# Attention and mixture-of-experts layer on one core: the value block at index 1 of each batch goes from one full-precision product to three rounded ones

## Chip, cores and metric

The kernel runs on one core of a Trainium2 chip (trn2). The metric is device time in microseconds (us); lower is better. Several executions of a kernel are timed and their median is taken. One further execution is profiled, and all rows below come from it.

## What is computed

The input `x` is 2 batches of 1024 tokens with 256 features (2048 tokens). Attention has 4 key/value groups with 4 query heads each, head size 128, rotary embedding and a causal mask. After it come a residual add and a layer norm, then a mixture of 64 experts (6 per token) with one shared expert, a residual add and a second layer norm. Cut to what matters here:

```python
q = einsum('bim,ghmd->bghid', x, w_aq); k = einsum('bim,gmd->bgid', x, w_ak)
v = einsum('bim,gmd->bgid', x, w_av)
s = einsum('bghid,bgjd->bghij', rope(q) * m, rope(k) * m) - 1e30 * (i < j)
o = einsum('bghij,bgjd->bghid', softmax(s), v)
x1 = layernorm(x + einsum('bghid,ghdm->bim', o, w_ao))
ids, w = grouped_topk(sigmoid(x1 @ gate_w) + bias)      # 6 of 64 experts
y = sum_k w_k * expert_k(x1) + silu(x1 @ ws_gate) * (x1 @ ws_up) @ ws_down
out = layernorm(x1 + y)
```

## The kernel before

**Stages.** Projections run from 0 to about 150 us: `x` is transposed, and each 128x512 piece of q, k and v is the sum of six rounded products (`ring`, `s_ps` and `o_ps` from `w_two` and `xt_hi`/`xt_lo`). q and k are rotated with two DVE products and one POOL instruction per piece, and stored to DRAM. Attention runs to about 915 us, then the experts and the final sum to 1071 us.

**Two precisions.** An fp32 operand can go through TensorE as it is (a product that the profile shows as two matmul records, here the line `L1143`), or be split into a rounded half (`_hi`, type fp32r, made by ACT in the helper at L875) and the rest (`_lo`, made by DVE in the helper at L1253 or by POOL). Three products of halves, hi by hi, lo by hi, hi by lo (`PASSES`), then stand for the full one.

**Attention in units.** A tile is 128 query tokens; there are 16 tiles, 8 to a batch. A unit is one tile and one group, so there are 64 units, numbered u = 4 x tile + group. A unit of tile i sees `blocks(u)` = i mod 8 + 1 blocks of 128 keys, and has 4 heads. For each head, PE makes the scores (`s_ps`), DVE takes their maximum (`neg_max`, L1319), ACT the exponential (`probs`, L961). For each key block j, the step (u, j) transposes the four heads' probabilities on PE (L1126, "ptrans") into a bank of `ring`, takes the bank out, and multiplies by the value block (L1143 or L1146, "pv") into `o_ps`, which holds one unit's sum. When the last block is in, DVE multiplies `o_ps` by the inverse row sums into `ot` (L1340, "omul"). There is one `o_ps` bank: the first pv of unit u waits until the omul of unit u-1 has read it (`o_ready`).

**The constant VF.** Value blocks j < VF = 2 of each batch are kept in full precision (`v0`, `v1`): ACT copies the transposed probabilities to `pt` (L972), that copy releases the bank, and PE makes the one full product (L1143). Blocks j >= VF have rounded halves in `v`: ACT makes `pt_hi`, DVE makes `pt_lo` (L1253), and the DVE instruction releases the bank; PE makes three products (L1146).

**The order.** `schedule()` writes one list of steps for all engines, and each engine walks it in order and issues its own part of each step. A step (u, j) is put in the list five heads behind the scores. `waiting` holds LAG = 2 pv steps: as soon as a third is in, the oldest is emitted. So this is emitted at the point that matters for u >= 1, j = 1:

```python
seq.append(("ptrans", u, j))       # (u, 1)
waiting.append((u, j))
if len(waiting) > LAG:
    product()                      # ("pv", u-1, last), and behind it ("omul", u-1)
```

Behind it come the scores of the next head, ptrans (u, 2), and pv (u, 0) (for a unit of two blocks ptrans (u+1, 0) in place of (u, 2)). For units with five or more blocks, steps (u, 0) and (u, 1) belong to one head, and the exponential of the head whose scores came just before is emitted between them; with two to four blocks (u, 1) stands before the exponential.

**Other work in the list.** The router, shared expert and norms of the previous tiles are put between heads by the table `BETWEEN`. The raw router and shared-expert weights wait in the memory of `v1` until they are split (`MISC_AT`). Values of the second batch are stored to DRAM during the projections (`v_out` to `v_rows`), loaded into `v` when the first batch is done with it (`load_v`, four loads, at omul 29 to 32), and split by ACT and POOL (`vsplit`, L829 on POOL). Expert weights are loaded during the second batch into the memory that `kt0`, `v0` and `kt1` leave (`load_homes`).

Of the kernel before, what the change touches and what calls it, by code (L numbers as in the profile page):

```python
# [10 lines left out]
F32 = mybir.dt.float32  # L11
# [4 lines left out]
P = 128  # L16

B, T, M = 2, 1024, 256
G, H, D = 4, 4, 128
NT = T // P  # L20
# [35 lines left out]
RING = 3  # L56
XB = 4
QB = 3
VF = 2
VS = NT - VF  # L60
PRE_BANKS = 8
BLOCKS = ["K", 0, 1, 2, 3, "V"]
# [200 lines left out]
PT_ALL = len(PT_AT)  # L263
PS_AT = {k: n for n, k in enumerate(k for k in PT_AT if k[1] >= VF)}
PROJ_AT = {s: n for n, s in enumerate(s for s in SEQ if s[0] in ("proj", "projv"))}
# [16 lines left out]
def build(nc, x, w_aq, w_ak, w_av, w_ao, gate_w, bias, w_gate, w_up, w_down, ws_gate, ws_up, ws_down,  # L282
# [9 lines left out]
    with ExitStack() as ctx:  # L292
        def sb(name, shape, dt, where=ctx):
            return where.enter_context(nc.sbuf_tensor(name, shape, dt))

        def sem(name):
            return ctx.enter_context(nc.semaphore(name))
# [22 lines left out]
        wsd_lo = sb("wsd_lo", [F, M], F32R)  # L320

        att = ExitStack()
        kt = [sb("kt0", [P, G, 2, T], F32R, att)]
        v_sb = [sb("v0", [P, G, VF, D], F32, att)]
        raw = ExitStack()
# [49 lines left out]

        v_sb.append(sb("v1", [P, G, VF, D], F32, att))
        x_sb = sb("x_sb", [P, XB, M], F32, att)
# [57 lines left out]
        wmisc_lo_ready = sem("wmisc_lo_ready")  # L435
# [110 lines left out]
            return tile.rearrange("p (y h d) -> p y h d", h=H, d=D // 2)  # L546

        kt_hi, kt_lo = [z[:, :, 0, :] for z in kt], [z[:, :, 1, :] for z in kt]
        raw_misc = v_sb[1][:, :, :, :].rearrange("p g n d -> p (g n d)")
        raw_r = raw_misc[:, 0:2 * M].rearrange("p (c n) -> p c n", c=MC)  # L550
        raw_d = raw_misc[0:F, 2 * M:3 * M]

# [2 lines left out]
        def load_k(eng, b, g):  # L555

            for z in range(2):
                eng.dma_start(kt_lo[b][z * D // 2:(z + 1) * D // 2, g, :].bitcast(F32),
                              rows_of[0, z, g * D // 2:(g + 1) * D // 2, b * T:(b + 1) * T]).then_inc(k_loaded, 16)

        def rope_done(eng, c, name):

            for n in range(2 * SETS):
                eng.wait_ge(rope_stored[n], 16 * len(range(n // 2, ropes_until(c, name), SETS)))
# [4 lines left out]
        def read(eng, step):  # L569

            r, turn = PLACE[step]
            eng.wait_ge(ring_read[r], turn + 1)

        def reader(ins, step):

            ins.then_inc(ring_read[PLACE[step][0]], 1)

        def bank(step):
            r = PLACE[step][0]
            if r < 4:  # L580
                return s_ps[:, r // 2, r % 2 * 512:r % 2 * 512 + 512]
            return o_ps[:, :] if r == 4 else ring[:, (r - 5) % RING, :]
# [4 lines left out]
        def used(eng, semaphore, n):  # L587

            if n > 0:
                eng.wait_ge(semaphore, n)  # L590
# [25 lines left out]
        def _(sp):  # L616
# [63 lines left out]
            for s in SEQ:  # L680
# [10 lines left out]
                if s[0] == "score" and s[1:] in K_LOAD_AT:  # L691
                    load_k(sp, 1, K_LOAD_AT.index(s[1:]))
                if s[0] == "projv" and s[1] >= NT + VF:
                    j = s[1] - NT - VF
                    read(sp, s)
# [176 lines left out]
        def _(act):  # L872
            def split(hi, raw):

                return act.activation(hi, raw, ACT.Copy)  # L875
# [10 lines left out]
            for s in SEQ:  # L886
                for name in HIGH_AT.get(s, []):
                    n = BLOCKS.index(name)
# [19 lines left out]
                if kind == "projv":  # L908
                    act.wait_ge(proj_ready, PROJ_AT[s] + 1)
                    b, j = divmod(s[1], NT)  # L910
                    rows = bank(s).rearrange("p (g d) -> p g d", g=G)
                    if j < VF:
                        if s[1] == NT:
                            act.wait_ge(wmisc_lo_ready, 2)
                        reader(act.activation(v_sb[b][:, :, j, :], rows, ACT.Copy), s)
                    elif b == 0:
                        split(v[:, :, 0, j - VF, :], rows).then_inc(v_hi_ready, 1)
                    else:
                        used(act, v_stored, 16 * (j - VF))
                        reader(act.activation(v_out[:, :], bank(s), ACT.Copy), s)  # L920
                if kind == "vsplit":
                    g = s[1]
                    act.wait_ge(v_loaded[g % 2], 16 * (g // 2 + 1))
                    split(v[:, g, 0, :, :], v[:, g, 1, :, :].bitcast(F32)).then_inc(v_later_hi, 1)
                if kind == "ksplit":
                    b, g = s[1:]
                    act.wait_ge(k_loaded, 32 * G * (b + 1))
                    split(kt_hi[b][:, g, :], kt_lo[b][:, g, :].bitcast(F32)).then_inc(k_hi_ready, 1)
                if kind == "proj" and s[1:] in BLANK_AT:
                    n = BLANK_AT.index(s[1:])  # L930
# [5 lines left out]
                if kind == "proj" and s[1] == CHUNKS // B - 1 and s[2] in (1, 2) and s[4] == 1:  # L936
                    rope_done(act, s[1], "K")
                    act.wait_ge(proj_ready, PROJ_AT[s] + 1)
                    load_k(act, 0, 2 * (s[2] - 1) + s[3])
                if s == ("proj", CHUNKS - 1, 1, 0, 0):  # L940
                    act.wait_ge(proj_ready, PROJ_AT[("proj", CHUNKS - 1, 0, 1, 1)] + 1)
# [10 lines left out]
                if kind == "exp":  # L952
                    u, h = s[1:]
                    n = u * H + h
# [9 lines left out]
                if kind == "ptrans":  # L964
                    n = PT_AT[s[1:]]
# [590 lines left out]
```

## Time and profile before

| | us |
|---|---|
| median of 3 runs | 1075.36 |
| lowest and highest of them | 1070.57, 1077.23 |
| the profiled execution's own time | 1073.27 |
| its span, first to last instruction | 1071.5 |
| mean granted TensorE clock in it | 0.957 of full |

The span leaves 1.8 us of the profiled execution's time outside, and that execution was 2.1 us faster than the median. In the rows, PE is TensorE's matmuls, DVE is VectorE, ACT is ScalarE, POOL is GpSimd. Matmuls overlap in the pipeline, so a step's cost on PE is read from start to start. What stands in brackets behind a row is idle time of the engine before it and what ended it.

### The profile page before, as it was taken

How to read it: one execution, taken by the hardware profiler on the slowest of the kernel's cores; microseconds unless marked ns; L12 is line 12 of the kernel's file. 1: busy time of each engine (PE TensorE's matmuls, PEld its weight loads, DVE VectorE, ACT ScalarE, POOL GpSimd, SP SyncE). 2: the span in 40 equal slices, each digit the busy share in tenths (PEclk: the TensorE clock that was granted, in tenths of full speed). 3: DMA queues.
4: the chain of work that ended last, by engine and by line, in shares of the span. 5: the costliest groups of instructions: out<-in, count | busy, mean ns of one | idle time of the engine just before them, and what ended most of it. 6: DMA issues, size and time to landing. Idle time of an engine off the chain costs nothing.

```text
span 1071.5 us, 16751 instructions
## 1 busy us (share of the span) xinstructions
PE 965.9 (90%) x5240; PEld 739.3 (69%) x5240; DVE 681.1 (64%) x1703; ACT 488.6 (46%) x1083; POOL 371.8 (35%) x334
## 2 busy tenths in 40 slices
PE   8999979989999999999979999999999998559745
PEld 6888867667787778776767667888787776336412
DVE  5989853775766675757565668575857666424326
ACT  4012124555656564645544456564645544125402
POOL 4878863234323121021244332312031112126811
PEclk9999988999999999999979999999999999769968
DMA  8696765463222111111243224351112133978687
GB/s 254 228 289 218 250 230 159 127 165 110 73 64 61 60 52 58 45 33 50 85 133 90 84 74 132 87 156 45 56 31 69 44 79 99 274 214 194 86 279 284
DMA packets 137303, 137.24 MB, mean 128 GB/s; under 512 B 18065, under 2 KB 108805, under 8 KB 137216
## 3 DMA queue, kind: packets, MB, share of 16 engines
q1 hardware_dynamic: 84064, 98.33, 30.1%
q10 hardware_dynamic: 43872, 29.50, 9.4%
q0 software_dynamic: 9280, 8.34, 4.5%
q8 instruction: 44, 0.72, 0.3%
q14 instruction: 43, 0.35, 0.1%
HBM read 86.44 MB, written 63.05 MB: 140 GB/s over the span
## 4 chain that ended last, share of the span: by engine, by line
PE 67%; DVE 10%; issue 8%; SPq 5%; DMA 5%; ACT 2%; POOL 2%; ACTq 1%; DVEq 0%; POOLq 0%
PE s_ps L1116 14%; PE ring L1126 9%; PE o_ps L1146 8%; PE o_ps L1143 8%; PE ring L1155 7%; PE s_ps L1095 6%; PE ring L1095 5%; DVE neg_max L1319 2%; SPq L759 2%; PE s_ps L1209 2%; PE o_ps L1095 2%; SPq L655 1%; PE s_ps L1119 1%; DVE pt_lo L1253 1%; DMA inverses<-inv_t 1%
## 5 line engine op out<-in xcount | busy, mean ns | idle before, releaser
L1319 DVE TENSOR_REDUCE neg_max<-s_ps 128x1 f32<-128x128 f32 (+7 forms) x256 | 191.6, 750 | 137.6 <-PE s_ps L1119 131.8
L961 ACT ACTIVATE probs<-s_ps,neg_max 128x128 f32<-128x128 f32 (+7 forms) x256 | 189.7, 741 | 142.3 <-DVE neg_max L1319 127.8
L1116 PE MATMUL s_ps<-kt,qt_hi 128*128 128x512 f32 (+3 forms) x768 | 235.2, 388 | 6.0 <-ACT probs L961 3.9
L824 POOL TENSOR_TENSOR qt_lo<-q_raw,qt_hi 128x512 fp32r<-128x512 f32 x64 | 82.1, 1283 | 319.3 <-ACT qt_hi L875 319.0
L1126 PE MATMUL ring<-ident,probs 128*128 128x128 f32 x1152 | 177.5, 277 | 9.2 <-DVE pt_lo L1253 5.1
L875 ACT ACTIVATE pt_hi<-ring 128x512 fp32r<-128x512 f32 x168 | 99.8, 596 | 181.8 <-PE ring L1126 173.6
L1116 PEld LDWEIGHTS s_ps<-kt,qt_hi 128*128 128x128 f32 x768 | 139.7, 194 | 54.9 <-issue 30.2
L1253 DVE TENSOR_TENSOR pt_lo<-ring,pt_hi 128x512 fp32r<-128x512 f32 x168 | 115.4, 687 | 62.2 <-ACT pt_hi L875 56.7
L1126 PEld LDWEIGHTS ring<-ident,probs 128*128 128x128 f32 x1152 | 129.1, 142 | 33.7 <-issue 14.5
L1146 PE MATMUL o_ps<-pt_hi,v 128*128 128x512 f32 x336 | 145.9, 435 | 1.4 <-DVE pt_lo L1253 0.9
L1116 PE MATMUL s_ps<-kt,qt_lo 128*128 128x512 f32 (+3 forms) x384 | 134.6, 350 | 0.0
L1143 PE MATMUL o_ps<-pt,v 128*128 128x512 f32 x240 | 127.8, 615 | 1.9 <-DVE ot L1340 1.7
L846 POOL DMA_INDIRECT slot_rows<-row,slot_u x96 | 95.1, 990 | 95.7 <-DVE slot_u L1444 73.5
L814 POOL TENSOR_TENSOR prods<-prods 128x512 f32<-128x512 f32 x80 | 108.6, 1385 | 36.6 <-DVE prods L1306 36.2
L1155 PE MATMUL ring<-wo,ot 128*128 128x256 f32 x512 | 113.1, 379 | 0.0
L1155 PEld LDWEIGHTS ring<-wo,ot 128*128 128x128 f32 x512 | 97.1, 190 | 17.5 <-issue 4.3
L972 ACT ACTIVATE pt<-ring 128x512 f32<-128x512 f32 x120 | 71.3, 594 | 26.4 <-PE ring L1126 20.0
L1116 PEld LDWEIGHTS s_ps<-kt,qt_lo 128*128 128x128 f32 x384 | 74.1, 193 | 8.4
L1340 DVE TENSOR_TENSOR ot<-o_ps,inv_row 128x512 f32<-128x512 f32 x64 | 43.9, 686 | 42.4 <-PE o_ps L1146 20.8
L1146 PEld LDWEIGHTS o_ps<-pt_hi,v 128*128 128x128 f32 x336 | 63.4, 189 | 9.5 <-DVE pt_lo L1253 1.7
L1146 PE MATMUL o_ps<-pt_lo,v 128*128 128x512 f32 x168 | 65.8, 392 | 0.0
L833 POOL TENSOR_TENSOR rstd<-var_eps,minus_half 128x1 f32<-128x1 f32 x16 | 9.1, 569 | 153.2 <-DVE var_eps L1352 153.2
(201 smaller groups left out, 1378.8 us busy)
## 6 DMA issues: line engine op xcount, KB each, us to landing
qk_rows<-prods SPq DMA_DIRECT2D x80, 256.0 KB, 2.8
q_raw<-qk_rows ACTq DMA_DIRECT2D x128, 128.0 KB
inv_row<-inverses SPq DMA_DIRECT2D x64, 256.0 KB
fsum<-sums SPq DMA_DIRECT2D x48, 256.0 KB, 8.1
sums<-blank SPq DMA_DIRECT2D x16, 640.0 KB
wexp<-in_L_ffn_w_gate_dram SPq DMA_DIRECT2D x32, 192.0 KB, 5.0
wexp<-in_L_ffn_w_up_dram SPq DMA_DIRECT2D x32, 192.0 KB, 5.2
wexp<-in_L_ffn_w_down_dram SPq DMA_DIRECT2D x32, 192.0 KB, 6.3
```

Of the source, the lines that this page charges most:

```text
L814: pool.tensor_tensor(pair[:, z, 0, :], pair[:, z, 0, :], pair[:, z, 1, :], op).then_inc(rot_ready, 1)
L846: pool.indirect_dma_start(slot_rows[:, :], bass.IndirectOffsetOnAxis(ap=slot_u[:, i % 2, k:k + 1], axis=0), row[:, i % 2, :], None, bounds ...
L875: return act.activation(hi, raw, ACT.Copy)
L961: act.activation(probs[:, u % 2, h, 0:blocks(u) * P], s_ps[:, n % 2, score_cols(n)], ACT.Exp, bias=neg_max[:, n % 8:n % 8 + 1], accum_out= ...
L1095: ins = pe.matmul(bank(s), *sides, start=(turn == 0), stop=(turn == len(PROJ_PASSES) - 1))
L1116: pe.matmul(s_ps[:, n % 2, c + a:c + e], q[qp], k[kp][:, a:e], start=(qp == kp == 0), stop=(qp == 1 and not last))
L1126: ins = pe.transpose(bank(s)[:, h * P:(h + 1) * P], probs[:, u % 2, h, j * P:(j + 1) * P], ident[:, :])
L1143: ins = pe.matmul(o_ps[:, :], v_sb[i // NT][:, g, j, :], pt[:, n % PTB, :], start=first, stop=last)
L1146: ins = pe.matmul(o_ps[:, :], v[:, g, vp, j - VF, :], (pt_hi, pt_lo)[pp][:, n % PTB, :], start=False, stop=(last and vp == 1))
L1155: ins = pe.matmul(bank(s)[:, 0:M], ot[:, h // H, (h % H) * P:(h % H + 1) * P], wo[:, h, :], start=(h == 0), stop=(h == G * H - 1))
L1253: return dve.tensor_tensor(lo, raw, hi.bitcast(F32), ALU.subtract)
L1319: dve.tensor_reduce(neg_max[:, n % 8:n % 8 + 1], s_ps[:, n % 2, score_cols(n)], AX_X, ALU.max, negate=True).then_inc(max_ready, 1)
```

## The change

`VF` becomes 1. Only value block 0 of each batch stays in full precision; block 1 is made of rounded halves and goes through the three products, as blocks 2 to 7 do. `v` holds seven blocks for each group in place of six, `v0` and `v1` one in place of two. `v1` is then too small for the raw router and shared-expert weights, so these are loaded into a tensor of their own that lies in the memory of `kt0`; the loads of the first batch's keys into `kt0` wait until the weights have been split, and the first copy into `v1` no longer does.

```diff
-VF = 2
+VF = 1
 VS = NT - VF
...
         att = ExitStack()
+        early = ExitStack()
+        raw_misc = sb("raw_misc", [P, 3 * M], F32, early)
+        early.close()
         kt = [sb("kt0", [P, G, 2, T], F32R, att)]
         v_sb = [sb("v0", [P, G, VF, D], F32, att)]
...
-        raw_misc = v_sb[1][:, :, :, :].rearrange("p g n d -> p (g n d)")
         raw_r = raw_misc[:, 0:2 * M].rearrange("p (c n) -> p c n", c=MC)
...
                     if j < VF:
-                        if s[1] == NT:
-                            act.wait_ge(wmisc_lo_ready, 2)
                         reader(act.activation(v_sb[b][:, :, j, :], rows, ACT.Copy), s)
...
                     rope_done(act, s[1], "K")
                     act.wait_ge(proj_ready, PROJ_AT[s] + 1)
+                    act.wait_ge(wmisc_lo_ready, 2)
                     load_k(act, 0, 2 * (s[2] - 1) + s[3])
```

The rest follows from `VF`. The lines of `build` behind the new ones stand a line lower after the change (L1253 is then L1254, L1340 is L1341).

**PE, unit 27.** The transposes of blocks 2 and 3 (`ring<-ident,probs`) and the products of blocks 0 and 1 (`o_ps<-...`) behind them. Before:

```order
1120 L1126 MATMUL ring<-ident,probs 128x128 x4
1121 L1143 MATMUL o_ps<-pt,v0 128x512
1122 L1126 MATMUL ring<-ident,probs 128x128 x4
1123 L1143 MATMUL o_ps<-pt,v0 128x512
1124 L1180 MATMUL ring<-chose,before_bf 128x64
```

The same place after the change:

```order
1166 L1127 MATMUL ring<-ident,probs 128x128 x4
1167 L1144 MATMUL o_ps<-pt,v0 128x512
1168 L1127 MATMUL ring<-ident,probs 128x128 x4
1169 L1147 MATMUL o_ps<-pt_hi,v 128x512
1170 L1147 MATMUL o_ps<-pt_lo,v 128x512
1171 L1147 MATMUL o_ps<-pt_hi,v 128x512
1172 L1181 MATMUL ring<-chose,before_bf 128x64
```

The product of block 1 is three instructions in place of one, at the same place.

**DVE, between units 26 and 27.** `neg_max` are score maxima, `inv_sum` and `inv_t` the inverse row sums of unit 27, `ot` the omul of unit 26, `chose_s` to `row` routing work. Before:

```order
615 L1319 TENSOR_REDUCE neg_max<-s_ps 128x1
616 L1325 RECIPROCAL inv_sum<-row_sum 128x4
617 L1326 STREAM_TRANSPOSE inv_t<-inv_sum 128x32
618 L1340 TENSOR_TENSOR ot<-o_ps,inv_row 128x512
619 L1415 SCALAR_TENSOR_TENSOR chose_s<-left,sig 128x64
620 L1418 TENSOR_REDUCE top_sum<-chose_s 128x1
621 L1419 RECIPROCAL top_inv<-top_sum 128x1
622 L1420 TENSOR_SCALAR row<-chose_s,top_inv 128x64
623 L1319 TENSOR_REDUCE neg_max<-s_ps 128x1
624 L1253 TENSOR_TENSOR pt_lo<-ring,pt_hi 128x512 x2
```

The same place after the change:

```order
641 L1320 TENSOR_REDUCE neg_max<-s_ps 128x1
642 L1326 RECIPROCAL inv_sum<-row_sum 128x4
643 L1327 STREAM_TRANSPOSE inv_t<-inv_sum 128x32
644 L1254 TENSOR_TENSOR pt_lo<-ring,pt_hi 128x512
645 L1341 TENSOR_TENSOR ot<-o_ps,inv_row 128x512
646 L1416 SCALAR_TENSOR_TENSOR chose_s<-left,sig 128x64
647 L1419 TENSOR_REDUCE top_sum<-chose_s 128x1
648 L1420 RECIPROCAL top_inv<-top_sum 128x1
649 L1421 TENSOR_SCALAR row<-chose_s,top_inv 128x64
650 L1320 TENSOR_REDUCE neg_max<-s_ps 128x1
651 L1254 TENSOR_TENSOR pt_lo<-ring,pt_hi 128x512 x2
```

One `pt_lo`, that of step (27, 1), stands in DVE's queue directly ahead of `ot`, the omul of unit 26. The same holds for 54 of the 56 units with two or more blocks (for units 5 to 31 and 37 to 63, not for units 4 and 36).

## Rows read from the trace of the kernel before

**Rows 1.** The page: each engine's busy time, PE and granted clock in 40 slices

```profile
PE 965.9 (90%) x5240; PEld 739.3 (69%) x5240; DVE 681.1 (64%) x1703; ACT 488.6 (46%) x1083; POOL 371.8 (35%) x334
PE   8999979989999999999979999999999998559745
PEclk9999988999999999999979999999999999769968
```

**Rows 2.** Busy time by stretch, tile 13: PE, PEld, DVE, ACT, POOL, clock, DMA

```profile
727.00:784.00 57.00, 56.17 (x317) 45.06 (x315) 39.33 (x88) 32.40 (x63) 11.67 (x11) 1.00 0.17 52
```

**Rows 3.** PE in order of time (start, length): full-precision steps of unit 30

```profile
507.19 0.61 PE L1126 MATMUL ring<-ident,probs 128*128 128x128 f32 x4
507.64 1.02 PE L1143 MATMUL o_ps<-pt,v 128*128 128x512 f32 x2
508.50 0.60 PE L1126 MATMUL ring<-ident,probs 128*128 128x128 f32 x4
```

**Rows 4.** PE in order of time: rounded steps of unit 57

```profile
809.95 0.61 PE L1126 MATMUL ring<-ident,probs 128*128 128x128 f32 x4
810.31 0.48 PE L1146 MATMUL o_ps<-pt_hi,v 128*128 128x512 f32 x1
811.09 0.60 PE L1126 MATMUL ring<-ident,probs 128*128 128x128 f32 x4
```

**Rows 5.** Groups by line and shape: busy us, mean ns, idle before and its releasers

```profile
L1253 DVE TENSOR_TENSOR pt_lo<-ring,pt_hi 128x512 fp32r<-128x512 f32 x168 | 115.4, 687 | 62.2 <-ACT pt_hi L875 56.7 <-issue 3.6
L875 ACT ACTIVATE pt_hi<-ring 128x512 fp32r<-128x512 f32 x168 | 99.8, 596 | 181.8 <-PE ring L1126 173.6 <-issue 5.2 <-PE o_ps L1143 2.4
L972 ACT ACTIVATE pt<-ring 128x512 f32<-128x512 f32 x120 | 71.3, 594 | 26.4 <-PE ring L1126 20.0 <-issue 5.7
```

**Rows 6.** In order of time, unit 27: ACT's copy of (27, 1), omul 26, pv (27, 0)

```profile
449.63 0.59 ACT L972 ACTIVATE pt<-ring 128x512 f32<-128x512 f32 x1
449.59 0.69 DVE L1340 TENSOR_TENSOR ot<-o_ps,inv_row 128x512 f32<-128x512 f32 x1 [0.77 <-PE o_ps L1146]
451.24 1.02 PE L1143 MATMUL o_ps<-pt,v 128*128 128x512 f32 x2
```

**Rows 7.** In order of time: from ACT's `pt_hi` over `pt_lo` to DVE's next instruction

```profile
429.14 0.59 ACT L875 ACTIVATE pt_hi<-ring 128x512 fp32r<-128x512 f32 x1
429.76 0.69 DVE L1253 TENSOR_TENSOR pt_lo<-ring,pt_hi 128x512 fp32r<-128x512 f32 x1 [1.05 <-ACT pt_hi L875]
430.37 1.33 DVE L1386 TENSOR_TENSOR biased<-sig,bias_sb 128x64 f32<-128x64 f32 x1
```

**Rows 8.** In order of time: an omul and the pv that waits for it

```profile
903.89 0.69 DVE L1340 TENSOR_TENSOR ot<-o_ps,inv_row 128x512 f32<-128x512 f32 x1 [1.35 <-issue]
904.73 1.10 PE L1143 MATMUL o_ps<-pt,v 128*128 128x512 f32 x2 [0.49 <-DVE ot L1340]
```

**Rows 9.** In order of time, unit 26: ACT's copy of (26, 1), omul 25, pv (26, 0)

```profile
437.02 0.59 ACT L972 ACTIVATE pt<-ring 128x512 f32<-128x512 f32 x1
436.24 0.67 DVE L1340 TENSOR_TENSOR ot<-o_ps,inv_row 128x512 f32<-128x512 f32 x1
437.31 1.02 PE L1143 MATMUL o_ps<-pt,v 128*128 128x512 f32 x2
```

**Rows 10.** In order of time, unit 9: ACT's copy of (9, 1) and pv (9, 0)

```profile
224.19 0.60 ACT L972 ACTIVATE pt<-ring 128x512 f32<-128x512 f32 x1
225.78 1.10 PE L1143 MATMUL o_ps<-pt,v 128*128 128x512 f32 x2
```

**Rows 11.** The omul line: who waited for it (us, times)

```profile
  PE o_ps L1143: 1.7, 3
```

**Rows 12.** Busy time by stretch, where DVE is full in tiles 1 and 9

```profile
195.00:210.00 15.00, 14.37 (x83) 9.81 (x83) 13.81 (x54) 9.63 (x28) 2.54 (x2) 1.00 0.57 151
584.00:597.00 13.00, 12.37 (x67) 8.33 (x66) 12.48 (x49) 8.56 (x25) 2.56 (x3) 1.00 0.36 101
```

**Rows 13.** Instructions on `v`: POOL's split (ns min/median/max, first and last start)

```profile
L829 POOL TENSOR_TENSOR v<-v x4: 1812/1824/1834, 533.3 to 563.5; 128x768 fp32r<-128x768 f32 x4
```

## Prediction

> **What bounds the kernel now.** I read the page first. PE is busy 90% of the span and its digit is 9 in nearly every slice of the attention, at a granted clock that reads 9 there; DVE is busy 64%, ACT 46% [rows 1]. The view by stretch says the same of a late tile: in 57.00 us PE works 56.17, DVE 39.33, ACT 32.40, and the clock is 1.00, the upper level of 2.4 GHz [rows 2]. So time on PE counts in full there, and other engines' time counts only where PE comes to wait for it. Then I read PE, ACT and DVE side by side in order of time around one place of each unit, because the change puts an instruction into DVE's queue there.
>
> **What PE saves.** A full-precision step is transposes and one product. From the start of its transposes to the start of the next ones it takes 508.50 - 507.19 = 1.31 us [rows 3]. A rounded step takes 811.09 - 809.95 = 1.14 us [rows 4]. That is 0.17 us less. The steps (u, 1) change, one for each unit with two or more blocks: 7 tiles x 4 groups x 2 batches = 56. So 56 x 0.17 = 9.5 us less on PE. The transposes in front of a full product also take longer to make way (0.45 against 0.36 us from their start to the product's); without that part the product alone goes from 508.50 - 507.64 = 0.86 to 811.09 - 810.31 = 0.78 us, and the saving is 4.5 us [rows 3, 4]. I take 9.5, which the whole step shows, and keep 4.5 as the other end.
> The Trainium skill's page "FP8 and Floating Point Precision", section "TensorE Precision Notes", says that true FP32 is four passes through the array; by this rule three rounded products would take three quarters of a full one, so 0.86 us would become 0.65 and 56 steps would save 12 us. The rows show 0.78, since the first of the three products takes 0.32 of it.
>
> **What ACT and DVE get.** ACT's instruction is the same size: `pt` 594 ns, `pt_hi` 596 [rows 5]. DVE gets 56 more `pt_lo` of 687 ns, 38.5 us, on 681 [rows 1, 5]. DVE has room for the sum. What matters is where they stand.
>
> **The wait that they make.** DVE's order changes to: `pt_lo` of (u, 1), then the omul of unit u-1. DVE works in order, so the omul now waits until ACT has taken out (u, 1) and `pt_lo` is done. Before, it waited only for the last product of unit u-1. And there is one `o_ps` bank: PE's pv (u, 0) waits for that omul. Between ptrans (u, 1) and pv (u, 0) PE has only the last product of u-1, one head's scores and ptrans (u, 2) to do.
> The new chain from the end of ACT's copy of (u, 1): `pt_lo` starts 0.03 us after it (429.14 + 0.59 = 429.73, then 429.76) and DVE's next instruction starts 0.61 after `pt_lo`'s start [rows 7]. The omul takes 0.69, and the pv that waits for it starts 0.15 behind its end (903.89 + 0.69 = 904.58, then 904.73) [rows 8]. Together 0.03 + 0.61 + 0.69 + 0.15 = 1.48 us.
> Unit 27 is a common case: ACT's copy ends at 449.63 + 0.59 = 450.22, so pv (27, 0) could start at 451.70. It started at 451.24: 0.46 us of waiting is new [rows 6]. That distance does not go away when PE is held, since ACT's copy stands behind the exponential, this behind `neg_max`, and this behind PE's own scores. In unit 9 (three blocks) the copy ends at 224.79 and pv starts at 225.78: 1.48 - 0.99 = 0.49 us new [rows 10]. In unit 26 DVE and ACT are late with routing work: the copy ends at 437.61, after pv (26, 0) had started (437.31): 1.48 + 0.30 = 1.78 us new [rows 9].
> I did this subtraction for the 54 units that have the new order. In 14 of them (all of tiles 1 and 9, and units at tile starts, behind the output projection) pv (u, 0) comes later than the chain: nothing. In 29 it costs 0.2 to 0.6, the first of them unit 9 and one more unit 27, mean 0.4: 11.5 us. In five (18, 20, 30, 50, 62) 0.6 to 1.0, mean 0.9: 4.5 us. In six (22, 26, 29, 54, 58, 61) 1.6 to 1.9, mean 1.75, unit 26 among them: 10.5 us. Sum 26.5 us. The waits for an omul that PE has today are 1.7 us in three places [rows 11], so nearly all of this is new.
> Bounds: if held PE lets the late engines catch up, so that the eleven dear units cost as much as the common ones, it is 40 x 0.4 = 16; a lower end of 13 leaves room for the misc chains in tiles 2 and 10 that wait for DVE anyway. If the later `neg_max` (DVE's omul moves by 0.6 to 2.2 us) also holds up scores, I allow 4 more, 30. I take 26.5.
> The Trainium skill's page "PSUM — Partial Sum Buffer", section "Engine vs sequencer instructions", says that the ScalarE and VectorE queues are strict FIFO. This is the rule that speaks against the change: without it the omul could pass `pt_lo`, the term of 26.5 us would be 0, and the sum would be the saving alone. The trace agrees with the rule as far as it goes: DVE stood idle for 1.05 us before a `pt_lo` that waited for ACT, and the instruction behind it came after it [rows 7].
>
> **DVE where it is full.** At the end of tile 1 and of tile 9 DVE works 13.81 of 15 us and 12.48 of 13 while PE works 14.37 and 12.37 [rows 12]. Of the eight new `pt_lo` of these tiles some fall there and cannot hide. All eight would be 8 x 0.61 = 4.9 us, none 0. Two or three fall in, so I take 1.5.
>
> **Edits at nothing.** In the first batch, ACT's copy of value block 1 becomes a split with one DVE instruction behind it (0.69 us, the size of `pt_lo` [rows 5]), during the weight loads, when DVE still waits for weights; without that cover it costs 0.7. One more `v_out` store goes through SP's queue during the projections, ahead of `prods` stores that DVE sometimes waits for; I allow 1 us and take 0. The loads of `v` carry seven blocks in place of six, and the splits of a group grow with them, on POOL from 1824 to some 2130 ns (7/6 by size). The last of them began at 563.5 us [rows 13]; the halves of the second batch are first read in tile 9 in place of tile 10, and tile 9's units lie in the second stretch of rows 12 and a little ahead of it, so some 10 us of cover are left; without it the four splits would cost 4 x 0.3 = 1.2. The new wait ahead of the key loads is for a split that stands earlier in the same list and that PE, DVE and ACT pass before them; if it were late, ACT's `xt_hi` copies behind it would be held, at most 1 us. One expert pair is loaded a few units later, whole tiles before it is used. I give all these 0, and -0.5 to +2 to the range.
>
> **Sum.** 1073.3 (the profiled execution) - 9.5 + 26.5 + 1.5 = 1091.8 us. The median of the runs was 2.1 above this execution, so a median may come out at up to 1094; I say 1092.
>
> **Rivals.**
> 1. *Part of the wait is swallowed.* The stall is real, but PE's delay gives DVE and ACT back what they were late, and waits that PE has anyway later in a tile shrink. For it: DVE idles a third of the time [rows 2]. Against it: the common case hangs on PE's own scores. With 13 in place of 26.5 and no full-DVE term: 1073.3 - 9.5 + 13 = 1076.8, no change that can be measured.
> 2. *The saving decides; not slower.* The mechanism: pv (u, 0) is not held, because `pt_lo` is done before the last product of u-1 is. It decides where ACT's copy of (u, 1) ends 1.5 us before pv (u, 0) starts. That is so in the 14 units counted above. If it were so in all, 1073.3 - 9.5 = 1063.8. Against it: rows 6, 9 and 10.
> 3. *By the page's four passes* the same case saves 12 and ends at 1061.3, which is the only one that is faster by over 1%. Against it the 0.78 us of rows 4.
> 4. *DVE becomes the bound.* The 38.5 us on DVE come out in full beside the saving: 1073.3 - 9.5 + 38.5 = 1102.3. Against it: 39.33 of 57 us busy [rows 2]. It could come by the chain of `neg_max`, exponential and scores, if DVE's shift in each unit is not won back.
>
> **How the numbers follow.** About 1% (10.8 us) is what a measurement of this kernel can tell from no change. The forecast (1083 to 1099 by its own bounds) gets 0.74, rival 1 0.13, rival 2 0.02, rival 3 0.03, rival 4 0.08. Slower by over 1% is the forecast and rival 4: 0.82. Within 1% is rivals 1 and 2: 0.15. Faster is rival 3: 0.03. The range from 1080 to 1101 takes the forecast's own range and most of rival 4, and leaves out under 2 in 10.
>
> **What would show it.** Right: in the new profile PE's idle time before the full product of block 0, put down to `ot`, grows from 1.7 us to over 15 (where a wait is short the records may show it as a longer transposes-to-product distance); in each of units 22, 26, 29, 54, 58 and 61 pv (u, 0) starts 1.4 to 1.5 us behind the end of ACT's copy of (u, 1); tiles 5 to 7 and 13 to 15 grow by about 2 to 3 us each, tiles 1 and 9 by 1 at most or shrink; `pt_lo` is x224; the steps (u, 1) take 1.14 us. Wrong: the omul line still releases PE in a few places only, or tiles get shorter by 0.7 us throughout, or the late tiles grow by much more than 3 us, which would be rival 4.

## The result and the profile after

| | before | after |
|---|---|---|
| median of 4 runs | 1076.08 us | 1102.52 us |
| lowest to highest | 1070.57 to 1077.23 | 1101.25 to 1104.41 |
| ratio to before, 95% interval | | 1.0257 [1.0227, 1.0286] |
| profiled execution (its span) | 1073.27 (1071.5) | 1101.25 (1099.4) |

The changed kernel is 26.4 us slower. The forecast was 1092.0 (1080 to 1101): the sign and the mechanism came out. The size did not: the time is 10.5 us above the forecast and 1.5 us above the range. One execution of experiment 10 below, at 1074.35 us and the lowest granted clock of its six, counts as slow and is left out of its median.

The page of the changed kernel: busy time of PE and DVE, PE and its clock in 40 slices, the chain of work that ended last by engine, and two groups (busy us, mean ns, idle time before them and its releasers).

```profile
PE 962.5 (88%) x5296; PEld 749.2 (68%) x5296; DVE 710.8 (65%) x1760; ACT 490.4 (45%) x1083; POOL 372.6 (34%) x334
PE   8999978889999899998978899999999998539835
PEclk9999989999999999999979999999999999859968
PE 49%; DVE 20%; issue 14%; SPq 6%; ACT 5%; DMA 3%; POOL 2%; ACTq 1%; POOLq 0%; DVEq 0%
L1254 DVE TENSOR_TENSOR pt_lo<-ring,pt_hi 128x512 fp32r<-128x512 f32 x224 | 154.0, 687 | 104.5 <-ACT pt_hi L877 103.5
L1144 PE MATMUL o_ps<-pt,v 128*128 128x512 f32 x128 | 71.6, 643 | 22.1 <-DVE ot L1341 21.6
```

The same row of the chain on the page of the kernel before:

```profile
PE 67%; DVE 10%; issue 8%; SPq 5%; DMA 5%; ACT 2%; POOL 2%; ACTq 1%; DVEq 0%; POOLq 0%
```

PE is drawn busy for 3.4 us less than before ([rows 1], 965.9) and the clock is the same 0.957 over the span; the span is 28 us longer. `pt_lo` is there 224 times in place of 168 [rows 5]. In the chain PE falls from 67% to 49% and DVE rises from 10% to 20%: the end is now often set by what PE waits for. The last row says what that is: before the full product of block 0 PE stood idle for 21.6 us until `ot` was done, where before it was 1.7 [rows 11]. A late tile, 13, from the end of its predecessor's last omul to that of its own:

```profile
743.00:803.40 60.40, 56.88 (x322) 46.16 (x322) 41.18 (x93) 32.38 (x64) 12.00 (x12) 1.00 0.16 49
```

Measured in this way the tile took 57.2 us before; [rows 2] show 57.0 of them. The granted clock is 1.00 in both, and PE's share falls from 56.17 of 57.00 to 56.88 of 60.40. No engine is full in it any more: part of the time goes by in a chain across engines.

One unit of it, in order of time (start, length, engine). Unit 27, which [rows 6] showed before:

```profile
455.43 0.59 ACT L877 ACTIVATE pt_hi<-ring 128x512 fp32r<-128x512 f32 x1
456.05 0.69 DVE L1254 TENSOR_TENSOR pt_lo<-ring,pt_hi 128x512 fp32r<-128x512 f32 x1 [1.43 <-ACT pt_hi L877]
456.58 0.61 PE L1127 MATMUL ring<-ident,probs 128*128 128x128 f32 x4
456.66 0.68 DVE L1341 TENSOR_TENSOR ot<-o_ps,inv_row 128x512 f32<-128x512 f32 x1
457.49 1.10 PE L1144 MATMUL o_ps<-pt,v 128*128 128x512 f32 x2 [0.30 <-DVE ot L1341]
458.42 0.60 PE L1127 MATMUL ring<-ident,probs 128*128 128x128 f32 x4
```

DVE stands idle for 1.43 us with the omul of unit 26 behind the `pt_lo` that waits. From the end of ACT's copy (456.02) to the product that overwrites `o_ps` it is 457.49 - 456.02 = 1.47 us, where 1.48 was forecast. PE's own work would have had the product start about 0.45 behind its transposes [rows 3], at 457.03; it starts 0.91 behind them: 0.46 us of waiting, the forecast's number for this unit. (The trace puts only 0.30 of it down to `ot`, because it draws the transposes as running until 457.19.) In the dear units the same chain costs more; unit 26:

```profile
440.95 0.61 PE L1127 MATMUL ring<-ident,probs 128*128 128x128 f32 x4
441.11 1.08 ACT L877 ACTIVATE pt_hi<-ring 128x512 fp32r<-128x512 f32 x2
441.73 0.69 DVE L1254 TENSOR_TENSOR pt_lo<-ring,pt_hi 128x512 fp32r<-128x512 f32 x1 [1.32 <-ACT pt_hi L877]
442.34 0.68 DVE L1341 TENSOR_TENSOR ot<-o_ps,inv_row 128x512 f32<-128x512 f32 x1
443.16 0.67 PE L1144 MATMUL o_ps<-pt,v 128*128 128x512 f32 x1 [1.60 <-DVE ot L1341]
```

PE's transposes start at 440.95, the product 2.21 later; without the wait it would be 0.45: 1.76 us, forecast 1.78. Read in this way over all units with the new order (start of transposes to start of product, after against before), the added waits come to 26.7 us, against the 26.5 of the forecast.

The waits of 26.7 less the saving of 9.5 do not make 28 us. Part of the rest stands in the view of PE's waits (line waited at, releaser: us in total, times, longest). Attention before, 165 to 915 us:

```profile
PE ring L1163 <- DVE row L1358: 5.9, 5, 1.8
PE ring L1180 <- DVE chose L1411: 5.2, 4, 2.3
PE ring L1126 <- DVE pt_lo L1253: 5.1, 7, 1.1
PE ring L1176 <- DVE hid L1378: 4.1, 2, 2.4
```

and after, 166 to 940.5 us:

```profile
PE o_ps L1144 <- DVE ot L1341: 21.6, 37, 1.7
PE ring L1181 <- DVE chose L1412: 8.3, 4, 3.0
PE ring L1177 <- DVE hid L1379: 7.4, 5, 3.2
PE ring L1164 <- DVE row L1359: 6.3, 5, 1.8
PE ring L1127 <- DVE pt_lo L1254: 5.9, 7, 1.1
```

The small products of the routing and the shared expert (`chose`, `hid`, `row`) waited for a late DVE before; they wait 8.3 + 7.4 + 6.3 = 22.0 in place of 5.9 + 5.2 + 4.1 = 15.2 us. All releasers but `ot` together (small ones not shown) went from 31.2 to 37.5: 6.3 us. Some 1.8 of it lie in tile 8, which has one block and no changed step, and whose waits are as much longer in experiment 2 below, which adds no work to DVE. 4.5 lie elsewhere, 1.3 and 1.4 of them in tiles 1 and 9. For all of this the forecast had 1.5.

### The profile page after: what moved, and what is told of

The parts are those of the page before. It is cut to its first block, busy times and chain, and to the rows that moved or that the text cites. A ratio compares the mean times of both kernels' runs of the same rounds, so it can differ in the third digit from the quotient of the medians.

```text
span 1099.4 us, 16924 instructions
## 1 busy us (share of the span) xinstructions
PE 962.5 (88%) x5296; PEld 749.2 (68%) x5296; DVE 710.8 (65%) x1760; ACT 490.4 (45%) x1083; POOL 372.6 (34%) x334
## 4 chain that ended last, share of the span: by engine, by line
PE 49%; DVE 20%; issue 14%; SPq 6%; ACT 5%; DMA 3%; POOL 2%; ACTq 1%; POOLq 0%; DVEq 0%
PE s_ps L1117 9%; PE ring L1156 7%; PE o_ps L1147 6%; DVE neg_max L1320 6%; PE s_ps L1096 5%; PE ring L1127 5%; PE ring L1096 5%; PE o_ps L1144 4%; ACT pt_hi L877 3%; DVE ot L1341 3%; DVE pt_lo L1254 2%; SPq L761 2%; SPq L657 2%; PE s_ps L1210 2%; PE o_ps L1096 2%
## 5 line engine op out<-in xcount | busy, mean ns | idle before, releaser
L1117 PE MATMUL s_ps<-kt,qt_hi 128*128 128x512 f32 (+3 forms) x768 | 225.8, 376 | 7.4 <-ACT probs L962 5.2
L1254 DVE TENSOR_TENSOR pt_lo<-ring,pt_hi 128x512 fp32r<-128x512 f32 x224 | 154.0, 687 | 104.5 <-ACT pt_hi L877 103.5
L877 ACT ACTIVATE pt_hi<-ring 128x512 fp32r<-128x512 f32 x224 | 132.9, 594 | 178.2 <-PE ring L1127 176.0
L1147 PE MATMUL o_ps<-pt_hi,v 128*128 128x512 f32 x448 | 196.4, 439 | 0.3 <-DVE pt_lo L1254 0.3
L1156 PEld LDWEIGHTS ring<-wo,ot 128*128 128x128 f32 x512 | 97.1, 190 | 15.2 <-issue 1.9
L1147 PEld LDWEIGHTS o_ps<-pt_hi,v 128*128 128x128 f32 x448 | 85.4, 191 | 10.6 <-DVE pt_lo L1254 1.0
L1144 PE MATMUL o_ps<-pt,v 128*128 128x512 f32 x128 | 71.6, 643 | 22.1 <-DVE ot L1341 21.6
L1147 PE MATMUL o_ps<-pt_lo,v 128*128 128x512 f32 x224 | 88.5, 395 | 0.0
L1120 PE MATMUL s_ps<-causal_bf,ident_bf 128*128 128x128 bf16 x256 | 60.1, 235 | 0.0
L861 POOL DMA_INDIRECT sums<-erow,goal_u x32 | 46.7, 1458 | 38.2 <-DVE dve_cell L1469 21.8
```

Source lines behind the costliest of these rows:

```text
L1117: pe.matmul(s_ps[:, n % 2, c + a:c + e], q[qp], k[kp][:, a:e], start=(qp == kp == 0), stop=(qp == 1 and not last))
L1144: ins = pe.matmul(o_ps[:, :], v_sb[i // NT][:, g, j, :], pt[:, n % PTB, :], start=first, stop=last)
L1147: ins = pe.matmul(o_ps[:, :], v[:, g, vp, j - VF, :], (pt_hi, pt_lo)[pp][:, n % PTB, :], start=False, stop=(last and vp == 1))
L1156: ins = pe.matmul(bank(s)[:, 0:M], ot[:, h // H, (h % H) * P:(h % H + 1) * P], wo[:, h, :], start=(h == 0), stop=(h == G * H - 1))
L1254: return dve.tensor_tensor(lo, raw, hi.bitcast(F32), ALU.subtract)
```

## The experiments

The theory after the result: (A) the place of the 54 `pt_lo` ahead of the omul costs 20 us or more, the 56 `pt_lo` as such cost a few us more where DVE is late, and the rounded product saves what the steps show. The rivals: (B) the added DVE work costs most of the time wherever it stands; (C) one of the other edits (the raw weights in the key tensor with its new wait, the second-batch halves) has a part in it. The ratios are to the kernel before, timed again beside each experiment, with their 95% intervals; they can differ from the quotient of the medians by up to 0.2%.

**1. The omul first.** The changed kernel, but DVE issues `pt_lo` of (u, 1) directly behind the omul of u-1 (in the 54 units with the new order); the work is the same.

```diff
-                if kind == "ptrans" and s[2] >= VF:
+                if kind == "ptrans" and s[2] >= VF and s[1:] not in HELD:
...
                     dve.tensor_tensor(ot[:, g, :], o_ps[:, :], inv_row[:, u % 2, :], ALU.mult).then_inc(o_ready, 1)
+                    if (u + 1, 1) in HELD:
+                        s = ("ptrans", u + 1, 1)
+                        n = PT_AT[s[1:]]
+                        dve.wait_ge(p_hi_ready, PS_AT[s[1:]] + 1)
+                        reader(low(pt_lo[:, n % PTB, :], bank(s), pt_hi[:, n % PTB, :]), s)
```

> The changed kernel, with DVE's pt_lo of step (u, 1) put directly behind the omul of unit u-1 in place of directly ahead of it (54 units). Nothing else differs: same instructions, same counts. Order theory (the 26.7 us of waits before pv (u, 0) come from that one place in DVE's queue): the waits go, the cheaper steps stay, a few us stay for DVE where it is full: 1068 to 1078 us. Load theory (DVE's 38 us more work is what costs, wherever it stands): 1095 us or more.

Measured: 1082.76 us, 1.0065 [1.0034, 1.0096]; 19.8 us of the 26.4 are gone. That is between the two theories' numbers, and 4.8 us above the upper end of the order theory's: the few us that were to stay are more. Unit 27 in order of time:

```profile
453.41 0.69 DVE L1343 TENSOR_TENSOR ot<-o_ps,inv_row 128x512 f32<-128x512 f32 x1
454.22 0.59 ACT L879 ACTIVATE pt_hi<-ring 128x512 fp32r<-128x512 f32 x1
454.61 0.61 PE L1129 MATMUL ring<-ident,probs 128*128 128x128 f32 x4
454.84 0.69 DVE L1256 TENSOR_TENSOR pt_lo<-ring,pt_hi 128x512 fp32r<-128x512 f32 x1 [0.74 <-ACT pt_hi L879]
455.05 1.02 PE L1146 MATMUL o_ps<-pt,v 128*128 128x512 f32 x2
455.91 0.49 PE L1129 MATMUL ring<-ident,probs 128*128 128x128 f32 x3
```

The omul no longer stands behind the copy, and the product follows its transposes by 0.44. It starts 0.24 behind the end of ACT's copy (454.81), so nothing but the queue had held it for 1.47. But the kernel is not faster than before: the rounded products and the DVE work are both still in it, and together they leave +0.65%.

**2. The raw weights' place alone.** `VF = 2` again, everything else of the change.

> The changed kernel with VF back at 2: of the change only the raw router weights' place in the first keys' memory is left, with the wait that moved. Both theories: 1073 to 1079 us, as before. A third theory (the place or the moved wait costs part of the 26 us, by the projections or the key loads): 1080 us or more.

Measured: 1075.16 us, 0.9989 [0.9966, 1.0013]. Tiles 2 to 7 and 9 to 15 of the profile are within 0.06 us each of before. That part of rival C has fallen. (The profiled execution was 8 us longer than the one before, in the projections, tiles 0, 1 and 8 and behind attention. These stretches vary by some us between the profiles of all kernels here; the other tiles repeat to a few hundredths.)

**3 and 4. The DVE work without the saving, at either place.** The kernel before, with a `pt_lo` of (u, 1) that nothing reads; the product stays one full product. In 3 it stands where the change has it, in 4 behind the omul.

```diff
-PS_AT = {k: n for n, k in enumerate(k for k in PT_AT if k[1] >= VF)}
+PS_AT = {k: n for n, k in enumerate(k for k in PT_AT if k[1] >= 1)}
...
-                    if s[2] < VF:
+                    if s[2] == 0:
                         reader(act.activation(pt[:, n % PTB, :], bank(s), ACT.Copy), s)
+                    elif s[2] < VF:
+                        act.activation(pt[:, n % PTB, :], bank(s), ACT.Copy).then_inc(p_hi_ready, 1)
...
-                if kind == "ptrans" and s[2] >= VF:
+                if kind == "ptrans" and s[2] >= 1:
```

> The kernel before, with the full-precision product kept for value block 1, but DVE makes a pt_lo of step (u, 1) as well (its result is not used) and releases the bank, at the place that the changed kernel has it: directly ahead of the omul. PE does what it did before. Order theory: all of the waits of the changed kernel and none of its saving: 1076 + 26.7 + 3 for the restart of the full product behind each wait + 3 where DVE is full = 1109 us (1104 to 1113), that is above the changed kernel by 5 to 9. If the rounded products themselves cost something that was not seen: below or at the changed kernel's 1102.

> As the run before it (full product for block 1, an unused pt_lo on DVE), but with that pt_lo directly behind the omul. It has DVE's 38 us of added work and neither the order nor the cheaper product. Order theory: 1076 to 1085 us, only what DVE's work costs where DVE is full. Load theory: 1100 us or more.

Measured: 3 takes 1105.04 us, 1.029 [1.022, 1.036]; 4 takes 1082.43 us, 1.0069 [1.0042, 1.0096]. Experiment 3 is 2.5 us above the changed kernel, where 5 to 9 were expected. Who waited for the omul, in 3:

```profile
  PE o_ps L1145: 21.6, 32
```

and in 4:

```profile
  PE o_ps L1147: 1.2, 2
```

With experiment 1 and the change this is a square:

| median, us | `pt_lo` ahead of the omul | behind it | the place |
|---|---|---|---|
| full product | 1105.04 (exp. 3) | 1082.43 (exp. 4) | 22.6 |
| three rounded products | 1102.52 (the change) | 1082.76 (exp. 1) | 19.8 |
| the rounding | -2.5 | +0.3 | |

The place costs 20 to 23 us whatever the product is, and rival B has fallen as the main cause. So has the rest of rival C: experiments 3 and 4 have none of the change's other edits and show both costs in full. The DVE work alone costs 1082.43 - 1076 = 6.5 us (by the interval 4.5 to 10.3). And the rounding, which the steps of PE price at 9.5, is worth 2.5 us in one column and nothing in the other. The intervals of experiments 1 and 4 leave that nothing open by some 4 us either way, and the 2.5 hangs on experiment 3, whose interval is over 7 us to each side; so the numbers speak against 9.5, but give no size.

**5. The omul first in the eleven dear units only** (18, 20, 22, 26, 29, 30, 50, 54, 58, 61, 62), a list in place of the rule for `HELD` in experiment 1. Do the waits add up one by one?

> The changed kernel with pt_lo put behind the omul in only eleven units, those in which the working before the change gave 0.6 us or more of waiting each (18, 20, 22, 26, 29, 30, 50, 54, 58, 61, 62), together 15 us. Order theory with each unit's wait standing for itself: 1102.5 - 15 - 11 x 0.07 = 1087 us (1083 to 1091). If the waits hang together (a wait that goes comes back in the next unit, or the late DVE only shows elsewhere): 1095 us or more.

Measured: 1095.37 us, 1.0182 [1.015, 1.0215], 7.2 us below the changed kernel, where 1083 to 1091 would be 11.5 to 19.5 below it. Waits for the omul:

```profile
  PE o_ps L1146: 11.8, 23
```

Unit by unit the waits of the eleven (14.9 us) are gone, but 23, 27, 42, 52, 55 and 59 wait 3.5 longer, and tile 7 gets shorter by 0.7 us only (69.2 to 68.5), though units 29 and 30 in it had 2.85 of the added waits. A part of a wait that is removed comes up at a later place: the miss is in the expectation that they were independent.

**6 and 7. Where the DVE work costs.** The unread `pt_lo` of experiment 4 in tiles 1, 7, 9 and 15 alone (16 of 56), and in the other tiles alone (40 of 56).

```diff
+def with_lo(u, j):
+    return j >= VF or j == 1 and u // G % NT in (1, 7)
...
-PS_AT = {k: n for n, k in enumerate(k for k in PT_AT if k[1] >= 1)}
+PS_AT = {k: n for n, k in enumerate(k for k in PT_AT if with_lo(*k))}
```

> As the run e4_lo_full_after (full product for block 1, unused pt_lo behind the omul), but that pt_lo is made only in tiles 1, 7, 9 and 15, 16 of the 56. It asks where DVE's added work costs. By the alignment of that run's PE with the kernel before, these four tiles hold 6.8 of its 9 us: 1081 to 1084 us. If the cost goes by the count of instructions: 1076 + 16/56 x 7 = 1078 us.

> The complement: the unused pt_lo behind the omul in the ten other tiles, 40 of 56. By the alignment: 2.3 us, so 1076 to 1080. If it goes by count: 1076 + 40/56 x 7 = 1081 us.

Measured: 1083.73 us, 1.0059 [1.0036, 1.0082] for the 16, and 1076.90 us, 1.0004 [0.9984, 1.0023] for the 40. In these two kernels nearly the whole cost of the DVE work lies in four of the fourteen tiles; the 40 instructions in the others cost 0.4 us, and by the interval at most 2.5, where a share by count would be 4.6. So the cost does not go by the count. Of the profiled tiles in 6, tile 15 is 2.7 us longer than before, tile 7 1.3 and tile 9 0.3; tile 1 varies too much between profiles to tell.

**8. Removing what makes ACT's copy late.** In the schedule a unit's exponential stands behind the first of the steps that fill a head's slot. ACT takes it ahead of the slot's later copies, and these come up to 1.1 us later for it. The edit, on the changed kernel, puts it behind all of them; `pt_lo` stays ahead of the omul.

```diff
             for _ in lagging(before):
-                if first:
-                    seq.append(("exp", u, h))
                 first = False
-        if first:
-            seq.append(("exp", u, h))
+        seq.append(("exp", u, h))
```

> The changed kernel, DVE's order as the change left it (pt_lo ahead of the omul), but in the list of steps the exponential of a head stands behind all transposes of that place instead of between the first and the second. ACT then takes (u, 1) out right after its transposes in units of five and more blocks, some 1.1 us earlier. The chain of copy, pt_lo, omul, pv is as long as before but starts earlier. Order theory: the waits of tiles 4 to 7 and 12 to 15 (23 of 26.7 us) go, those of tiles 2, 3, 10 and 11 stay, and exponentials that come later cost 0 to 6 us: 1078 to 1088 us. If instead the pt_lo's place alone decides and not when ACT is done: 1100 us or more.

Measured: 1069.90 us, 0.9941 [0.991, 0.9972], 32.6 us below the changed kernel and 8 us below the range expected. Unit 27:

```profile
450.93 0.60 PE L1124 MATMUL ring<-ident,probs 128*128 128x128 f32 x4
451.56 0.60 ACT L874 ACTIVATE pt_hi<-ring 128x512 fp32r<-128x512 f32 x1 [0.53 <-PE ring L1124]
452.06 1.11 ACT L959 ACTIVATE probs<-s_ps,neg_max 128x1024 f32<-128x1024 f32 x1
452.19 0.69 DVE L1251 TENSOR_TENSOR pt_lo<-ring,pt_hi 128x512 fp32r<-128x512 f32 x1 [0.65 <-ACT pt_hi L874]
452.80 0.68 DVE L1338 TENSOR_TENSOR ot<-o_ps,inv_row 128x512 f32<-128x512 f32 x1
453.52 0.61 PE L1124 MATMUL ring<-ident,probs 128*128 128x128 f32 x4
453.96 1.02 PE L1141 MATMUL o_ps<-pt,v 128*128 128x512 f32 x2
```

The copy now starts 0.63 behind its transposes and ahead of the exponential, and the chain of 0.03 + 0.61 + 0.69 + 0.15 ends before PE wants the bank. The order in DVE's queue is still that of the change: its price was the lateness of the copy that it made the omul wait for. PE's idle time put down to the omul falls from 21.6 to 5.6 us, and by the starts on PE the added waits fall from 26.7 to 4.7, of which 3.3 are in tiles 2, 3, 10 and 11, as expected. That is 22 of the 32.6; the other 10.6 are about what the next run shows the same edit to give where the change is not made.

**9. The same edit on the kernel before** (five rounds).

> The kernel before (value block 1 in full precision) with the exponential of a head behind all transposes of its place, as in e8_exp_behind. It tells what the change itself is worth under the better order. Theory A (the late tiles' gain of e8, 12 us by the alignment, is the order's own, and the change still costs a little: 4.7 us of waits before pv (u, 0) and DVE where it is full, against 9 us of cheaper steps): 1064 to 1068 us, below e8's 1070. Theory B (the gain came from the rounded steps once nothing waited for them): 1072 to 1077 us, above e8.

Measured: 1062.81 us, 0.9866 [0.9835, 0.9897], 13.2 us below the kernel before and the lowest median of all kernels here. Its waits in attention, 166 to 900 us, all that are over 2 us:

```profile
PE ring L1173 <- DVE hid L1375: 6.4, 3, 3.0
PE ring L1160 <- DVE row L1355: 5.9, 5, 1.8
PE ring L1177 <- DVE chose L1408: 5.2, 4, 2.6
PE o_ps L1140 <- DVE ot L1337: 2.5, 3, 1.5
PE ring L1167 <- issue: 2.5, 4, 0.8
```

The 5.1 us in seven places in which PE's transposes waited for a ring bank that `pt_lo` had not yet left are gone from the view. Tiles 7 and 15 lose 3.3 and 3.8 us, tiles 6 and 14 1.5 each, tiles 5 and 13 1.1 each.

**10 and 11. The rounded block 1 on that schedule**: with `pt_lo` behind the omul in all 54 units (10), and in the ten units only in which experiment 8 still waits (11).

> The changed kernel with both: exponential behind, and pt_lo of (u, 1) behind the omul in all 54 units. Order theory: the 4.7 us of waits that e8 has left go, 1065 to 1069 us. If a held pt_lo now only makes later steps wait for their bank or their product: 1070 us or more.

> As e11, but pt_lo behind the omul only in the ten units in which e8 still waits by 0.33 us or more (9, 10, 11, 14, 31, 41, 42, 43, 46, 63). Together 4.3 us of waits: 1065 to 1068 us, at or a little below e11, since the other units' banks are released as early as in e8.

Measured: 1063.94 us, 0.9868 [0.9829, 0.9907], and 1063.61 us, 0.9869 [0.9835, 0.9903]. Both are about 1 us below their expected ranges, as experiment 9 is. On a schedule that hides its `pt_lo` the second rounded block is worth nothing that these runs can tell from zero: experiments 9 and 11 differ by 0.8 us, with intervals of over 3 us to each side.

## Why the prediction was right and wrong

- **The mechanism and its price were right.** The chain of 1.48 us was measured at 1.47 in 37 of the 40 units that now wait and at 1.60 in the other three, and the sum of the added waits is 26.7 for 26.5. What made it exact was that each unit's distance was subtracted from rows rather than a mean taken. Experiments 1, 3 and 4 show the place in DVE's queue to be the cause. The Trainium skill's "PSUM — Partial Sum Buffer", section "Engine vs sequencer instructions", with its strict FIFO queues, was the rule to go by. The trace agrees: in unit 27 DVE stood idle for 1.43 us with the omul behind the `pt_lo` that waited. The bound of 16 for "held PE lets the late engines catch up" did not come into play: the six dearest units stayed at 1.6 to 1.85 us each.
- **The step that failed most: the term "DVE where it is full".** It had 1.5 us, of two or three `pt_lo` that fall into two full stretches [rows 12]. Experiment 4 measures 6.5 us for the DVE work alone, and in the changed kernel PE's waits for releasers other than the omul grow by 6.3 us, 4.5 without tile 8. Tiles 1 and 9 have 2.7 of the 4.5; the other 1.8 lie in tiles that the term did not have. Its mistake was to look for DVE's busy share alone and not for the places where PE already waited for DVE, 15.2 us for `row`, `chose` and `hid` before the change. These waits are no sure price either: 5.9 of the 15.2 lie in tile 8, which has no changed step, and tile 2, which has 3.1, gets 0.3 us longer in experiment 7. Nor is the cost always in the same place: without the wait for the omul it is largest in tiles 7 and 15 (experiment 6), but in the changed kernel the other waits of these two tiles do not grow. Why is not shown.
- **The term "What PE saves" was too large.** The rounded step takes 1.13 us (below), 1.14 was forecast. Of the 56 steps 49 are 0.16 to 0.17 us shorter, 7.9 in all; behind the other seven PE waits for DVE, and they save nothing. So 9.5 came to 7.9.
- **A term at nothing: the restart.** The products that waited for `ot` take longer themselves: 458.42 - 457.49 = 0.93 to PE's next start in unit 27, against 0.86 [rows 3] and against 455.91 - 455.05 = 0.86 in experiment 1, where it does not wait. That is so in 34 units which did not wait before, 2.5 us that no term held.

The rounded step (30, 1) in the changed kernel:

```profile
517.35 0.60 PE L1127 MATMUL ring<-ident,probs 128*128 128x128 f32 x4
517.70 0.48 PE L1147 MATMUL o_ps<-pt_hi,v 128*128 128x512 f32 x1
518.02 0.40 PE L1147 MATMUL o_ps<-pt_lo,v 128*128 128x512 f32 x1
518.25 0.39 PE L1147 MATMUL o_ps<-pt_hi,v 128*128 128x512 f32 x1
518.48 0.61 PE L1117 MATMUL s_ps<-kt,qt_hi 128*128 128x512 f32 x2
```

- **The mended sum**, from PE's starts in the two profiles laid side by side: 1073.3 - 7.9 + 26.7 + 2.5 + 6.2 = 1100.8, beside 1101.25 for the profiled execution. The 6.2 is all else by which attention on PE became longer, the waits just named above all; 0.45 lie outside attention. The range was too narrow for its own terms: the saving's other end 4.5, the waits' 30 and the full DVE's 4.9 give 1073.3 - 4.5 + 30 + 4.9 = 1103.7, but its upper end held the saving at 9.5.
- **The edits at nothing.** Experiment 2 shows no cost of the raw weights' place and their wait. The second batch's halves were not tried alone; no wait for the v splits is in PE's view of waits, and experiments 3 and 4, which have none of these edits, come within 2.5 us of their partners in the square.
- **The rivals.** Rival 1 did not come: the added waits were there in full (in experiment 5, though, 3.5 us of 14.9 came up again elsewhere). The condition of rival 2 held in the 14 units counted for it, where the added wait is 0.00. Rival 4 gave 1102.3, which is nearest to the measured time, but for a reason that is not there: experiment 7 adds 40 of the 56 `pt_lo` and costs 0.4 us. Its number and the right one meet by chance. Rival 3, by the four passes of the Trainium skill's "FP8 and Floating Point Precision", section "TensorE Precision Notes", needed 0.65 us for three rounded products; they take 518.48 - 517.70 = 0.78, as in [rows 4].
- **The signs named beforehand.** The wait for `ot` over 15 us: 21.6. The product 1.4 to 1.5 behind the copy: yes. Tiles 5 to 7 and 13 to 15 longer by 2 to 3 us: by 3.1, 3.3 and 1.9, and 3.1, 3.3 and 2.9. Tiles 1 and 9 longer by 1 at most: tile 9 by 0.5, tile 1 by 1.5, but experiment 7, which adds nothing in tile 1, has it 1.9 longer, so this sign says little.

## What to carry to other kernels

Where an engine that works in order is given a new instruction, first look at what stands behind it, who waits for that, and when the new instruction's own input is ready; 54 instructions of 0.69 us on an engine that idles a third of the time cost 20 us by their place, and 6.5 us by their work, nearly all of it in a few tiles. So look for the cost of added work on a second engine at the places where the bound engine waits for it today, not in its share of busy time; how much it costs there these waits do not say. And when such a chain is too long, ask which instruction makes its input late: moving the exponential behind the copies took away 22 of the 26.7 us of added waits, and gave the kernel before 13 us too.

## What the runs showed that was not expected

- A full product that starts after a wait takes longer than the same product behind running work: 0.93 to 0.94 against 0.86 us to the next start, drawn as 1.10 in place of 1.02 us, in units 27 and 30 of the changed kernel. Its 34 such units come to 2.5 us, and those of experiment 3 to 2.5 as well.
- The gain of the rounded product vanishes in the medians (+0.3 and -2.5 us in the square, +0.8 between experiments 9 and 11), though 49 steps on PE are 0.16 to 0.17 us shorter in every pair. From experiment 4 to experiment 1 these steps save 7.9 us, but PE's attention is only 1.2 us shorter, since 6.4 come up again between other instructions. From experiment 9 to experiment 10 tiles 5 to 7 and 13 to 15 are 0.63 to 0.72 us shorter each, as four steps should make them, but tile 4 is 1.25 longer, with PE waiting 1.5 us for ACT's `probs` in it, and tile 9 1.05 longer, with 1.4 us more of waits, 0.8 of them behind DVE. Why the two nearly cancel is not shown.
- PE's share of busy time in the page fell from 90% to 88% only, while the time grew by 2.6%: the drawn ends of matmuls cover short waits. The distance between starts on PE shows them, and so does the share of the other engines in the chain that ended last.
